# A state-space layer on one core: state sums by accumulating transposes, and seven states of the first direction read out by GpSimd

## The reference: what is computed

```
xp, z = split(x @ W_in.T)                    # 384 channels each
xc = silu(conv(xp) + conv_b)                 # 4 taps along the tokens
dt, Bt, Ct = split(xc @ W_xproj.T)           # 12, 16 and 16 columns
dt = softplus(dt @ W_dt.T + b_dt)
h[d, n] = exp(dt * A[d, n]) * h[d, n] + dt * xc * Bt[n]     # a scan over the tokens
y[d] = sum over n of h[d, n] * Ct[n]  +  D[d] * xc[d]
out = (y * silu(z)) @ W_out.T
```

## Time and profile before

| what | value |
|---|---|
| median of 3 runs | 4592.76 us |
| lowest and highest run | 4589.97 and 4595.15 us |
| the profiled execution's own time | 4601.28 us |
| its span, first to last instruction | 4599.5 us |
| mean granted TensorE clock over the span | 0.949 |
| state-space layer | roughly from 1160 to 3760 us of the span |

### The profile page before, as it was taken

How to read it: one execution, slowest core, us unless ns; L and a number is a source line. 1 busy time by engine, 2 the same in 40 slices (tenths; PEclk the granted TensorE clock), 3 DMA queues, 4 the chain that set the end, 5 groups by cost and what they waited for, 6 DMA issues and landing times. The chain is left out here.

```text
span 4599.5 us, 63372 instructions
## 1 busy us (share of the span) xinstructions
PE 4145.6 (90%) x17184; PEld 2234.8 (49%) x17184; DVE 3250.3 (71%) x5016; ACT 2413.6 (52%) x4880; POOL 3215.3 (70%) x1671
## 2 busy tenths in 40 slices
PE   7988958996999999999999999999999974999994
PEld 5666646672344344344334434433433434666773
DVE  5777762121899999999899999999989986112124
ACT  3566632223766766666676666667667544222221
POOL 3233213441999999999999999999999971444441
PEclk7999987997999999999999999999999987999997
DMA  1000023451343333433333333333333321344466
GB/s 34 25 21 23 15 64 87 122 151 52 108 119 116 120 112 112 124 112 120 120 115 112 112 115 121 113 115 116 122 112 115 111 85 49 109 117 118 134 185 227
DMA packets 264754, 478.66 MB, mean 104 GB/s; under 512 B 37044, under 2 KB 174084, under 8 KB 264548
## 3 DMA queue, kind: packets, MB, share of 16 engines
q1 hardware_dynamic: 235776, 403.02, 27.8%
q0 software_dynamic: 28032, 73.17, 6.4%
q10 hardware_dynamic: 740, 0.49, 0.0%
HBM read 409.60 MB, written 41.81 MB: 98 GB/s over the span
## 5 line engine op out<-in xcount | busy, mean ns | idle before, releaser
L1818 POOL TENSOR_TENSOR m_xh<-m_u,m_Bb 128x1536 f32<-128x1536 f32 x512 | 1776.9, 3539 | 58.1 <-DVE m_u L1689 44.9
L1745 PE MATMUL bank<-m_xh,ident 128*128 128x512 f32 x3072 | 1459.7, 611 | 36.3 <-POOL m_xh L1807 36.3
L1787 DVE TENSOR_TENSOR_SCAN bank<-bank,m_xh 128x512 f32<-128x512 f32 x864 | 1039.0, 1216 | 45.1 <-ACT bank L1774 41.9
L1774 ACT ACTIVATE bank<-m_dt,m_Ac 128x508 f32<-128x508 f32 x1536 | 1024.7, 683 | 38.4 <-DVE m_xh L1787 38.4
L1745 PEld LDWEIGHTS bank<-m_xh,ident 128*128 128x128 f32 x3072 | 577.2, 194 | 828.6 <-issue 737.1
L1787 DVE TENSOR_TENSOR_SCAN m_xh<-bank,m_xh 128x512 f32<-128x512 f32 x672 | 787.7, 1207 | 71.5 <-ACT bank L1774 66.0
L1807 POOL TENSOR_TENSOR m_xh<-m_xh,m_Cb 128x1536 f32<-128x1536 f32 x224 | 791.2, 3532 | 4.8 <-DVE m_xh L1787 4.5
L1798 DVE TENSOR_TENSOR m_xh<-bank,m_Cb 128x512 f32<-128x512 f32 x864 | 580.8, 672 | 9.8 <-DMA m_Cb<-BC_rows 9.8
L1204 ACT ACTIVATE f1t_h<-bank,f1t_b 128x512 f32<-128x512 f32 (+1 forms) x276 | 142.8, 589 | 471.3 <-PE bank L1239 471.3
L1593 PE MATMUL bank<-m_xp,m_dg 128*128 128x512 f32 x768 | 352.4, 601 | 3.7 <-DVE m_u L1689 1.4
L1134 POOL DMA_INDIRECT rows_y<-f1t_y,f1t_home x142 | 140.3, 988 | 272.7 <-DVE f1t_y L1175 243.4
(11 more groups left out here) (367 smaller groups left out, 6002.0 us busy)
## 6 DMA issues: line engine op xcount, KB each, us to landing
m_Bb<-BC_rows SPq DMA_DIRECT2D x256, 512.0 KB, 4.9
m_Cb<-BC_rows SPq DMA_DIRECT2D x256, 512.0 KB, 4.1
f1t_w<-f_w SPq DMA_DIRECT2D x46, 576.0 KB
m_r<-m_dt POOLq DMA_DIRECT2D x32, 768.0 KB, 7.4
f1t_w1a<-f_w SPq DMA_DIRECT2D x46, 384.0 KB
f0t_w<-f_w SPq DMA_DIRECT2D x22, 576.0 KB
f1c_yg<-rows_y SPq DMA_DIRECT2D x16, 768.0 KB, 8.3
f1t_w1b<-f_w SPq DMA_DIRECT2D x92, 96.0 KB
```

What stands on the lines that cost most here:

```text
L1745: mm = pe.matmul(bank[:, c, :], K.ident[:, :], xh[n % NX][:, c, :], start=False, stop=(d == 1 and n == NS - 1))
L1774: act.activation(o[:, :, lo:hi], seqs(dt[d][:, c, :])[:, :, lo:hi], ACT.Exp, scale=Ac[:, c, n:n + 1]).then_inc(s_dA, 1)
L1787: dve.tensor_tensor_scan(o, bank[:, RING[d][p], way], xh[n % NX][:, c, way], 0.0, ALU.mult, ALU.add).then_inc(s_h, 1)
L1818: pool.tensor_tensor(xh[n % NX][:, :, :], u[d][:, :, :], Bb[q % RB][:, n % QN, :].unsqueeze(1).to_broadcast([P, DC, TOK]), ALU.mult).then_ ...
```

## The change

PE sums by transposes: the read-out of a block is cut into four pieces of 128 tokens; each is loaded as the stationary matrix and multiplied by the identity in transpose mode, accumulating. The sums therefore stand in PSUM with the tokens on the partitions; piece j of block c has a place of its own in three banks. D * xc is added in that layout too: four products of 128 columns in place of one of 512. When all sums of a group are there, ACT copies the three banks to SBUF (`act_yt`, into `dt[1]`) and PE turns them back (`pe_yT`, twelve transposes), and DVE's gated products wait for that. D of the next group's first direction may open the banks only when all three gated products are made.

POOL reads out states 0, 3, 5, 8, 10, 13, 14 of the first direction, no longer 0, 3, 4, 5, 10, 12, 13, 14. The places move: gated products to 6, 7, 8 and D for d = 0 to 9, 10, 11; the last nine sums of a group are issued three to a unit at the first three units of the next.

```diff
-            "y": (6, 7, 9), "pe_D0": (14, 15, 17), "pe_D1": (6, 16, 25), "pe_out": (17, 18), "out": (14, 15),
+            "act_yt": (6, 6, 7), "pe_yT": (4, 5, 5), "y": (6, 7, 8), "pe_D0": (9, 10, 11), "pe_D1": (6, 16, 25), "pe_out": (17, 18), "out": (14, 15),
-        BY_POOL = (0, 3, 4, 5, 10, 12, 13, 14), (0, 6, 9, 10, 11, 14)
+        BY_POOL = (0, 3, 5, 8, 10, 13, 14), (0, 6, 9, 10, 11, 14)
+        yt = dt[1]
+        def place(j, c):
+            return divmod(j * DC + c, G)
+        def sums(j, c):
+            b, k = place(j, c)
+            return bank[:, b, k * P:(k + 1) * P]
         def pe_D(pe, g, d, c):
             pe.wait_ge(s_xc, g * 2 + d + 1)
             if d == 0 and later(g):
-                pe.wait_ge(s_gy, (g - 1) * DC + c + 1)
+                pe.wait_ge(s_gy, g * DC)
...
-            pe.matmul(bank[:, c, :], dgD[:, c, :], xc[d][:, c, :], start=(d == 0), stop=False).then_inc(s_D, 1)
+            for j in range(G):
+                b, k = place(j, c)
+                opens = d == 0 and c == 0 and (j == 0 or b != place(j - 1, c)[0])
+                mm = pe.matmul(sums(j, c), xc[d][:, c, j * P:(j + 1) * P], dgD[:, c, :], start=opens, stop=False, skip_group_check=True)
+            mm.then_inc(s_D, 1)
         def pe_sum(pe, g, d, n, c):
...
-            mm = pe.matmul(bank[:, c, :], K.ident[:, :], xh[n % NX][:, c, :], start=False, stop=(d == 1 and n == NS - 1))
+            for j in range(G):
...
+                mm = pe.matmul(sums(j, c), xh[n % NX][:, c, j * P:(j + 1) * P], K.ident[:, :], start=False, stop=closes,
+                               is_transpose=True, skip_group_check=True)
             mm.then_inc(s_red, 1)
+        def act_yt(act, g, b):
+            act.wait_ge(s_red, (g + 1) * 2 * UNITS)
+            act.copy(yt[:, b, :], bank[:, b, :]).then_inc(s_yt, 1)
+        def pe_yT(pe, g, c):
+            pe.wait_ge(s_yt, (g + 1) * DC)
+            for j in range(G):
+                b, k = place(j, c)
+                mm = pe.transpose(bank[:, c, j * P:(j + 1) * P], yt[:, b, k * P:(k + 1) * P], K.ident[:, :])
+            mm.then_inc(s_yT, 1)
         def dve_y(dve, g, c):
-            dve.wait_ge(s_red, (g * 2 * NS + 2 * NS - 1) * DC + c + 1)
+            dve.wait_ge(s_yT, g * DC + c + 1)
         def sums_at(carry):
...
-                begun = sum(p >= at for at in POS["pe_D0"])
-                if carry and begun < DC:
-                    upto = min(upto, begun)
-                now = list(range(done, min(upto, done + 2)))
+                if carry:
+                    begun = sum(p >= at for at in POS["pe_D0"])
+                    upto = min(3 * (p + 1) - LAG * DC, 0) if begun < DC else upto
+                now = list(range(done, min(upto, done + 3)))
```

More of the change, by code:

```diff
@@ L1449, in mamba_phase @@
         s_gy, s_ops, s_out = sem("gated_ready"), sem("outps_ready"), sem("res_ready")
+        s_yt, s_yT = sem("sums_copied"), sem("sums_turned")
+        yt = dt[1]
[4 more added lines that the diff above has]
+            return bank[:, b, k * P:(k + 1) * P]
         def seqs(t):
@@ L1744, in pe_sum @@
                 pe.wait_ge(s_prp, pool_reads(g, d, n + 1))
-            mm = pe.matmul(bank[:, c, :], K.ident[:, :], xh[n % NX][:, c, :], start=False, stop=(d == 1 and n == NS - 1))
+            for j in range(G):
+                closes = d == 1 and n == NS - 1 and c == DC - 1 and (j == G - 1 or place(j, c)[0] != place(j + 1, c)[0])
+                mm = pe.matmul(sums(j, c), xh[n % NX][:, c, j * P:(j + 1) * P], K.ident[:, :], start=False, stop=closes,
+                               is_transpose=True, skip_group_check=True)
             mm.then_inc(s_red, 1)
+        def act_yt(act, g, b):
[7 more added lines that the diff above has]
+            mm.then_inc(s_yT, 1)
         def pe_out(pe, g, i):
@@ L1915, in main @@
                     carry = d == 0 and later(g)
+                    if carry:
+                        for c, at in enumerate(POS["pe_yT"]):
+                            if at == p:
+                                pe_yT(pe, g - 1, c)
                     if carry and p in POS["pe_D0"]:
@@ L1930, in after @@
                             pe_sum(pe, NG - 1, 1, n, c)
+                    for c in range(DC):
+                        pe_yT(pe, NG - 1, c)
                     for i in two:
@@ L1938, in main, with after @@
                     act_decay(act, g, d, p)
-                program(act, "act", main, lambda act: None, lambda act: None)
+                    if d == 0 and later(g):
+                        for b, at in enumerate(POS["act_yt"]):
+                            if at == p:
+                                act_yt(act, g - 1, b)
+                def after(act):
+                    for b in range(DC):
+                        act_yt(act, NG - 1, b)
+                program(act, "act", main, lambda act: None, after)
             @block.gpsimd
```

## The result

The kernel after takes 4710.42 us (median of four runs, 4709.61 to 4712.49), the kernel before beside it 4591.74: ratio 1.0258, 95% interval 1.024 to 1.0276. So it is 119 us slower, where 47 was forecast: the sign and the range hold, the size is two and a half times too small. The profiled execution is 4709.61, its span 4707.9.

What follows compares the result with a forecast made beforehand. POOL was taken to bound the kernel, partly through DVE's waits. Afterwards DVE's 152.5 us of work plus 14.0 of waits give 166.5 a group, +3.0: +45 over 15 groups, +2 at the end, less 8.5: 4640 us (4540 to 4715).

Steps and rivals of the forecast that it cites:

- POOL -3.4: One read-out fewer on POOL in the first direction: 3.4 us less a group, so POOL would need 160.1.
- DVE's work +1.8: Three more read-outs on DVE in the first direction, 0.59 each: 1.8 us a group, for 152.5 of work.
- A sum at 0.47: Four transposes on PE make a sum in 0.47 us, where two 512-column records took 0.86.
- Gated products -1.5: DVE's wait at the gated products falls from 1.85 to 0.35 us a group, last sums being issued three to a unit.
- The order of D +5.2 (3.3 to 8.0): First-direction projection queues behind two D products on PE; DVE waits 5.2 us a group for decay 11.
- The transfer -2.0: PE's waits for POOL's accumulating transfer, 4.4 us a group, shrink; DVE's waits fall by 2.0 (0 to 4.4).
- the softplus products -1.5: Shorter sums queued ahead of later softplus products cut DVE's wait of 4.0 us a group by 1.5 (0 to 4.0).
- the second direction's share: Part of the transfer term: in the second direction only what POOL now lags at its start would go.
- The convolution behind the last sums +1.0 (0 to 2.5): Second convolution follows last sums that wait for POOL's last read-out, delaying ACT and decays: 1.0 us a group.
- 96 sums cost PE about 37 us less: Sums by transposes relieve PE of about 37 us a group; nothing waits for most of that.
- the faster rival: POOL's saved 3.4 us come through, 160.1 us a group: 4544 us, chance 0.32.
- The rival of the low clock: PE stays at the lower clock, D and projection at 1.2 GHz: 174.3 us a group, 4757 us, chance 0.07.

Runs made afterwards that it cites:

- e5: Kernel before with only the new list of seven POOL read-outs in the first direction: 4604.81 us, ratio 1.0013.
- e1: Kernel after with first-direction D moved to units 11, 12, 13, behind the projection: 4662.36 us, ratio 1.0145.
- e17: e13 with first-direction D back at units 9, 10, 11, ahead of the projection: 4618.33 us.
- e6: Kernel before with gated products at units 6, 7, 8 and first-direction D at 9, 10, 11, waiting for all three gated products: 4748.35 us.
- e13: e9 with more products of zeros in PE's other idle stretches, in both directions: 4578.88 us, ratio 0.9965.
- e14: Kernel after, order unchanged, with 14 products of zeros ahead of the sums of state 14: 4701.53 us.
- e15: e1 with 14 products of zeros, second convolution not moved: 4605.46 us.
- e11: e9 with POOL reading out state 13 in place of 14 in the second direction: 4654.94 us.
- e3: Kernel after with the projection ahead of D and block 1 of the second convolution ahead of the state 14 sums: 4673.18 us.
- e9: e3 with 14 products of zeros in PE's idle stretch ahead of the second convolution's block 1: 4608.58 us, ratio 1.0024.
- e8: Kernel after with one product of zeros, 128 columns, ahead of every sum: 4782.44 us.
- e4: Kernel after with sums by plain fp32 products with the identity instead of transposes: 4902.29 us.
- e18: e13 with 8 more products of zeros ahead of the second direction's projection: 4585.96 us.

## Why the prediction was right in sign and wrong in size

By its own terms, in us a group (means of twelve groups; where a unit is named, DVE's idle time ahead of it):

- *POOL -3.4*: its work fell by 3.0 (160.0 to 157.0), but its waits rose from 3.4 to 13.7. e5 shows that even without the new sums the read-out saved turns into idleness. The 160.1 that POOL was said to need was never reached.
- *DVE's work +1.8*: 2.0. Right. *A sum at 0.47*: 0.45. Right.
- *Gated products -1.5*: 1.88 to 0.37, exactly that.
- *The order of D +5.2 (3.3 to 8.0)*: 4.34 at unit 11, so right, with its cause: D and projection ran after 4.63 of idleness at a clock of 0.63. e1 takes it away and gains 3.3 a group; e17 puts it back and loses 2.7. e6's +9.6 shows how far it can go.
- *The transfer -2.0 and the softplus products -1.5*: together -3.3, near their sum, with the shares wrong. PE no longer waits for the transfer in the first direction, as forecast, and DVE's waits for softplus products went from 4.1 to 0.4. **But the second direction's share failed**: at its unit 31 the wait went from 2.92 to 3.35. POOL issues that transfer 0.9 earlier than before (42.7 instead of 43.6 behind the direction's first scan), yet it lands 8.2 us after its issue where it took 7.4 (medians), and so hardly earlier than before (50.9 and 51.1 behind that scan). Why it takes longer was not found. That product ran at the lower clock in both kernels (2.05 in the earlier trace rows); in e13 it takes 1.10 and the wait is 2.45.
- *The convolution behind the last sums +1.0 (0 to 2.5)*: **failed**, 3.13. It was priced at 3.61, full speed. PE stood idle 5.17 for POOL's read-out, so the sums took 1.35 more and the convolution 1.3 more. e14, which only fills that idleness, brings the wait to 0.62; the queue's order, which the term was about, makes little of it (e15).
- *Missing from the sum, so put at nothing*: units 16 to 31 of the first direction, 0.49 to 2.86. These are dt and gate products at 2.07 instead of 1.1, and e13 makes the wait vanish.

Waits were to grow by 1.2 and grew by 5.2. The missing 4.0 are 2.1 at the convolution and 2.4 at units 16 to 31, less 0.9 that D cost under its price; 0.4 are left for the transfer and small waits elsewhere.

The step that failed is thus the clock: the prediction asked it of one term, D, and priced the convolution, dt and gate products, as far as it counted them, at full speed. It made the low clock a rival of all or nothing, with a chance of 0.07 and a time of 4757. The truth lies between: the granted clock is 0.87 over the layer, lost stretch by stretch, in the group shown behind 5.17 and 4.63 us of idleness and again where PE worked in short pieces. So the signs of both came: the projection behind two D products and DVE's wait at decay 11, and a lower clock with waits spread over the group. "96 sums cost PE about 37 us less; nothing waits for most of that" was true of the work and false of its effect: with the old sums PE was busy for 578 of 600 us at a clock of 0.99.

Filling the idle stretches with products of zeros, with the projection ahead of D, takes 4662 to 4579 (e1 to e13). With that the new kernel comes out a little below the old one, though far from the faster rival's 4544. That the new sums and the seven read-outs earn this is not shown: the kernel before was not tried with such products, and its product behind the transfer ran at the lower clock too.

The rival of the low clock got a small chance because transposes had been seen to raise the clock. The rows here agree. In the kernel after, sums alone (16 and then 26 records, all transposes) ran in these stretches:

```profile
2295.75 6.27 PE L1760 MATMUL bank<-ident,m_xh 128*128 128x128 f32 x40
```

```profile
2296.00:2299.00 3.00, 3.00 (x16) 3.00 (x15) 1.79 (x2) 3.00 (x6) 2.65 (x2) 0.50 0.39 142
2299.00:2302.00 3.00, 3.00 (x26) 2.78 (x24) 3.00 (x4) 2.15 (x4) 3.00 (x2) 0.95 0.66 208
```

The clock rose behind transposes, from 0.50 to 0.95, as in the earlier trace rows. Ahead of them PE had made one product, behind 3.54 us of idleness; in the earlier trace rows more products had run, up to 36.67, so this case is the cleaner one. The Trainium skill (TensorE: Matmul & The Clock Gate, Part 4) says that the full clock does not engage for transpose mode; by that rule it would have stayed at the lower level here. The measurement decides against it.

What stays open: why the zeros gain at most 9 us in e14, with D in front, and 57 with the projection in front (e1 to e15); why the transfer of the second direction takes 0.8 longer; why state 13 in place of 14 costs (e11); and D in front with TensorE at full clock, and the kernel before with products of zeros, were not tried.

## What to carry to other kernels

Before taking work from TensorE, look at what its load does for its clock: where PE will stand idle ahead of a product that others wait for (here 4.3 to 5.2 us ahead of convolution and D), that product may run at the lower clock, and every such term has to be priced at both levels. Products with zeros in exactly those idle stretches can pay (here 1.4% between e3 and e9), while one ahead of every sum cost 72 us (e8). And a step that has its input early should not stand in a queue behind one that waits for another engine.

## What the runs showed that was not expected

- In e4, e8 and e18, PE stood idle for 2 to 5 us at the head of the hardware loop for nothing that the profile shows, in 13, 26 and 8 cases in the layer; in the rows of e8 and e18 the convolution records behind it took 5.52 and 5.18, instead of 3.6. In e13, with 16 records a group fewer than e18, it never did. What decides this was not found.
- The zeros of e9 cost nothing that can be seen: 28 records in 3.29 us in a stretch that was idle before.
